# Decoder layer with contextual position attention: logits halved between transposes, distances on ScalarE, the window in the ring banks

## The reference, cut to what matters

```python
sim = einsum('bid,bjd->bij', q, k) * d ** -0.5
G = sigmoid(sim)
P = flip(cumsum(flip(G, -1), -1), -1)          # sum of the gates from here to the last key
P = minimum(P, 63)
E = einsum('bnc,ct->bnt', q, pos_emb)          # 64 table entries for each query
w = P - floor(P)
sim = sim + w * take(E, ceil(P)) + (1 - w) * take(E, floor(P))
out = einsum('bij,bjd->bid', softmax(sim), v)
```

## Time and profile before

| | us |
|---|---|
| median of 3 runs | 2650.29 (2649.49 to 2651.93) |
| profiled execution, its own time | 2652.94 |
| its span, first to last instruction | 2651.1 |
| mean granted TensorE clock | 0.985 |

### The profile page before, as it was taken

One profiled execution on the slowest core, in us unless ns is written; L12 is line 12 of the kernel. 1 busy time (PEld: TensorE's weight loads), 2 busy tenths in 40 slices (PEclk: granted clock), 3 DMA queues, 4 the chain that ended last, 5 costly groups with the idle time before them and its releaser, 6 DMA issues. The chain is left out here.

```text
span 2651.1 us, 64197 instructions
## 1 busy us (share of the span) xinstructions
PE 2472.1 (93%) x18687; PEld 1691.1 (64%) x18687; DVE 2006.4 (76%) x5179; ACT 1615.9 (61%) x3383; POOL 190.4 (7%) x289
## 2 busy tenths in 40 slices
PE   7999998999899989998999999999999988999997
PEld 5666665666566656666666566666666656777776
DVE  6888888888888888888888888888899960232322
ACT  4666666666666666666666666666666663444442
POOL 0000000000000000000000000000000000111111
PEclk9999999999999999999999999999999998999998
DMA  2010101010101010100101110101001002100100
GB/s 68 20 33 20 34 20 32 20 34 20 32 20 34 20 32 21 32 21 21 29 24 29 25 29 24 29 24 29 22 21 40 21 17 68 34 26 34 36 26 6
DMA packets 96567, 74.74 MB, mean 28 GB/s; under 512 B 24590, under 2 KB 92303, under 8 KB 96464
## 3 DMA queue, kind: packets, MB, share of 16 engines
q1 hardware_dynamic: 96464, 73.15, 10.1%
HBM read 14.26 MB, written 2.10 MB: 6 GB/s over the span
## 5 line engine op out<-in xcount | busy, mean ns | idle before, releaser
L748 DVE TENSOR_REDUCE mx<-Sc 128x1 f32<-128x1024 f32 x512 | 621.5, 1214 | 160.2 <-PE Sc L544 159.7
L552 PE MATMUL ring<-ident,probs 128*128 128x128 f32 x4096 | 620.9, 284 | 115.2 <-ACT attn L418 65.3
L409 ACT ACTIVATE probsT<-ring 128x512 f32<-128x512 f32 x1024 | 584.7, 596 | 132.1 <-PE ring L552 129.2
L552 PEld LDWEIGHTS ring<-ident,probs 128*128 128x128 f32 x4096 | 446.3, 145 | 258.3 <-ACT attn L418 127.0
L430 ACT ACTIVATE probs<-Sc,nbias 128x1024 f32<-128x1024 f32 x512 | 565.6, 1117 | 4.7 <-DVE nbias L765 4.7
L544 PE MATMUL Sc<-qk,q_now 64*128 64x512 f32 x2048 | 539.4, 637 | 22.4 <-issue 16.0
L566 PE MATMUL out<-probsT,V_now 128*64 128x128 f32 x8192 | 530.0, 277 | 0.0
L566 PEld LDWEIGHTS out<-probsT,V_now 128*64 128x64 f32 x8192 | 439.5, 137 | 76.3 <-ACT probsT L409 57.9
L712 DVE COPY_PREDICATED z<-mask,z 128x224 f32<-128x224 int16 (+5 forms) x768 | 389.7, 507 | 34.4
L418 ACT ACTIVATE attn<-ring,rsum 128x64 f32 (+1 forms) x256 | 80.3, 314 | 436.5 <-PE ring L575 420.7
L544 PEld LDWEIGHTS Sc<-qk,q_now 64*128 64x128 f32 x2048 | 173.6, 188 | 217.8 <-issue 217.8
(11 more groups left out here) (116 smaller groups left out, 2301.8 us busy)
## 6 DMA issues: line engine op xcount, KB each, us to landing
q_now<-qk SPq DMA_DIRECT2D x256, 64.0 KB, 2.0
xv<-xT SPq DMA_DIRECT2D x113, 128.0 KB, 2.2
q_far<-qk SPq DMA_DIRECT2D x128, 64.0 KB, 1.9
V_now<-V SPq DMA_DIRECT2D x16, 512.0 KB, 3.2
at<-attn SPq DMA_DIRECT2D x16, 512.0 KB, 3.2
probs<-in_x_dram SPq DMA_DIRECT2D x4, 512.0 KB, 5.3
wqk<-in_L_attn_Wq_dram SPq DMA_DIRECT2D x32, 64.0 KB, 2.1
xin<-in_x_dram SPq DMA_DIRECT2D x16, 128.0 KB, 2.8
```

What stands on the lines that cost most here:

```text
L409: nc.scalar.activation(probsT[:, u, 4 * s:4 * s + 4, :], ring[k % 2][:, :].rearrange("p (t q) -> p t q", q=P), ACT.Copy).then_inc(slot_out, 1)
L552: last = nc.tensor.transpose(ring[k % 2][:, j * P:(j + 1) * P], probs[:, u, (4 * s + j) * P:(4 * s + j + 1) * P], ident[:, :])
L748: nc.vector.tensor_reduce(mx[:, u, half:half + 1], Sc[:, half * HALF:(half + 1) * HALF], AX.X, ALU.max).then_inc(dve_unit, 1)
```

## The change

1. **TensorE's order.** In each half of the body: half of the unit's logits, two sets of transposes (they need only the first half of the previous unit's exponentials), the other half of the logits, the turn, two more sets (`early_half`, `turn_and_late_half`).
2. **Banks.** `near` is gone. The window's two matmuls write the two ring banks, in front of unit 1's first logits, and wait until both are empty; the transposes behind them wait until ScalarE has read both. The turn gets a bank of its own (`turns`, with semaphores `turned` and `scaled`), so a body has 10 ring slots instead of 12.
3. **The window's operands.** Query tile 0 stays on array rows 64 to 127, tile 1 moves to rows 0 to 63, against a copy of the window's keys and table (`k_near`, loaded once a head, in its second body). `q_far` is two loads of 128 columns instead of one of 256.
4. **The distances.** ScalarE computes 1 + tanh (`steps`), after VectorE's scan the rounded position (`positions`) and the int16 distance (`distances`), three 128x352 operations. VectorE loses the rounding, the two floor scans, the distance and the clamp, and one of two last shifts; it gains one int16 mask (`even`). The fraction is taken from the even position.
5. **The table.** ScalarE writes it into `near_table_in`; GpSimd copies that to `z` (128x352), once the correction of the pair before is made (`start_table`).
6. **VectorE's order.** The shifts 6 to 2 now stand together ahead of unit 1's maxima instead of between them. At a head, SyncE issues `q_far` ahead of `V_now` instead of behind it.

```diff
-        near = pb("near", [P, BANK])
-        ring = [pb(f"ring{i}", [P, BANK]) for i in range(2)]
+        rings = pb("rings", [P, 2, BANK])
+        ring = [rings[:, i, :] for i in range(2)]
         out = pb("out", [P, BANK])
+        turns = pb("turns", [P, BANK])
...
-        near_win = near[:, 0:2 * (W + T)].rearrange("p (i w) -> p i w", w=W + T)[:, :, 0:W]
-        near_E = near[:, 0:2 * (W + T)].rearrange("p (i w) -> p i w", w=W + T)[:, :, W:W + T]
+        near_win = rings[:, :, 0:W]
+        near_E = rings[:, :, W:W + T]
...
-                sp.dma_start(q_far[C:P, :], queries(h, odd, t)).then_inc(far_in, 16)
+                for i in range(2):
+                    rows = slice(0, C) if i else slice(C, P)
+                    sp.dma_start(q_far[rows, :], queries(h, odd, t, i)).then_inc(far_in, 16)
+
+            def load_near(h):
+
+                sp.dma_start(k_near[:, h % 2, 0:W], qk[C:P, h % 2, 1, HALF - W:HALF]).then_inc(k_near_in, 16)
...
+            def start_table(c):
+
+                pool.wait_ge(near_out, c * 2 + 2)
+                if not (isinstance(c, int) and c == 0):
+                    wait_apart(pool, corr_done, c, waited)
+                nc.gpsimd.tensor_copy(z[:, 0, :, :], near_table_in[:, :, :]).then_inc(z_in, 1)
...
-            def near_table(c):
-                nc.scalar.activation(z[:, 0, :, W - T:W], near_E, ACT.Copy).then_inc(near_out, 1)
+                                     near_win, ACT.Tanh, scale=-0.5).then_inc(near_out, 1)
+
+            def steps(c):
+
+                act.wait_ge(near_out, c * 2 + 1)
+                nc.scalar.activation(passed[:, :, :], tanh[:, :, :], ACT.Identity,
+                                     bias=bias_one[:, :]).then_inc(step_in, 1)
+
+            def positions(c):
+
+                act.wait_ge(scanned, c * SC + SC)
+                nc.scalar.activation(rnd[:, :, :], behind[:, :, :], ACT.Identity, scale=TO_STEPS,
+                                     bias=bias_rnd[:, :]).then_inc(rounded, 1)
+
+            def distances(c):
+
+                act.wait_ge(rounded, c + 1)
+                nc.scalar.activation(dist[:, :, :], rnd[:, :, :], ACT.Identity, scale=2.0,
+                                     bias=bias_dist[:, :]).then_inc(dist_in, 1)
+
+            def near_table(c, first=False):
+                if not first:
+                    wait_apart(act, z_in, c, waited)
+                nc.scalar.activation(near_table_in[:, :, W - T:W], near_E, ACT.Copy).then_inc(near_out, 1)
...
-                at = Slots(first, proj)
+                at = Slots(proj)
+                if near:
+                    positions(g + 1)
                 if not first:
 
                     empty_halves(g - 1, 0)
-                    scale(g - 1, 0, base, at.turn0)
+                if near:
+                    distances(g + 1)
+                if not first:
                     transposed(1, base, at.last)
-                if near:
-                    act.wait_ge(corr_done, g + 1)
-                    near_table(g + 1)
+                    scale(g - 1, 0)
                 exps(g, 0)
-                if not first:
-                    empty_halves(g - 1, 1)
                 if proj:
                     project(g + PAIRS, not odd, base, at.qk, alone=not val)
                 if val:
                     values(g, base, at.values)
                 if not first:
-                    scale(g - 1, 1, base, at.turn1)
+                    empty_halves(g - 1, 1)
+                if far:
+                    near_tanh(g + 2)
+                    near_table(g + 2)
+                    steps(g + 2)
                 transposed(0, base, at.now)
-                if far:
-                    act.wait_ge(scanned, g * SC + (SC + 2))
-                    near_tanh(g + 2)
+                if not first:
+                    scale(g - 1, 1)
                 exps(g, 1)
...
                 for i in range(2):
-                    last = nc.tensor.matmul(near[:, i * (W + T):(i + 1) * (W + T)], q_far[C:P, i * P:(i + 1) * P],
-                                            qk[C:P, par, 1, HALF - W:QK], start=True, stop=True)
+                    rows = slice(0, C) if i else slice(C, P)
+                    keys = k_near[:, par, :] if i else qk[C:P, par, 1, HALF - W:QK]
+                    last = nc.tensor.matmul(rings[:, i, 0:W + T], q_far[rows, :], keys,
+                                            start=True, stop=True)
...
-            def turn(g, u, base, k):
+            def turn(g, u, evicted=True):
 
                 pe.wait_ge(halves_out, g * 2 + u + 1)
-                pe.wait_ge(slot_out, base + k - 1)
-                nc.tensor.matmul(ring[k % 2][:, 0:C], halves[:, u, :], fold[:, :],
-                                 start=True, stop=True).then_inc(slot_full, 1)
-
-            def body(g, odd, par, late=False, first=False, proj=True, val=True, far=True, far_par=None):
+                if evicted:
+                    wait_apart(pe, scaled, g * 2 + u, waited)
+                nc.tensor.matmul(turns[:, 0:C], halves[:, u, :], fold[:, :],
+                                 start=True, stop=True).then_inc(turned, 1)
+
+            def early_half(u, base, slots):
+
+                for s in range(2):
+                    transposes(u, base, slots, s)
...
+            def turn_and_late_half(g, u, base, slots, turned_unit, first=False, evicted=True):
+
+                if not first:
+                    turn(g, turned_unit, evicted)
+                for s in range(2, 4):
+                    transposes(u, base, slots, s)
...
                 logits(par, 0, 0)
                 if not first:
+                    early_half(1, base, at.last)
                     wait_apart(pe, exp_done, g * 4, waited)
                 logits(par, 0, 1)
                 if not first:
-                    turn(g - 1, 0, base, at.turn0)
-                    for s in range(4):
-                        transposes(1, base, at.last, s)
+                    turn_and_late_half(g - 1, 1, base, at.last, 0, evicted=not second)
                     outputs(g - 1, 1, base, at.last, tiles=range(FIRST))
                 if proj:
                     weights_at = (g // PAIRS) * 64 + 128 if val else H * 64 - 16
...
+                if far:
+                    wait_apart(pe, slot_out, base + at.now[0], waited)
+                    window(g + 2, par if far_par is None else far_par)
                 wait_apart(pe, exp_done, g * 4 + 1, waited)
                 logits(par, 1, 0)
+                if far:
+                    wait_apart(pe, near_out, g * 2 + 6, waited)
+                early_half(0, base, at.now)
                 wait_apart(pe, exp_done, g * 4 + 2, waited)
                 logits(par, 1, 1)
-                if not first:
-                    turn(g - 1, 1, base, at.turn1)
-                for s in range(4):
-                    transposes(0, base, at.now, s)
-                if far:
-                    pe.wait_ge(near_out, g * 2 + 4)
-                    window(g + 2, par if far_par is None else far_par)
+                turn_and_late_half(g - 1, 0, base, at.now, 1, first)
                 outputs(g, 0, base, at.now, empty=not first)
...
-            def round_positions(c):
+            def saturation(c):
 
                 after_scan(c, "scan 1")
-                nc.vector.tensor_scalar(rnd[:, :, :], twoP[:, :, :], 2.0 * T - 3.0, RND2,
-                                        ALU.min, ALU.add).then_inc(scanned, 1)
-                nc.vector.tensor_tensor(satmin[:, :], satmin[:, :], twoP[:, :, 0], ALU.min)\
-                    .then_inc(ramped, 1)
-
-            def scan_floors(c):
-
-                after_scan(c, "round")
-                for i in range(2):
-                    nc.vector.tensor_tensor_scan(flo[:, i, ::-1], twos[:, :], rnd[:, i, ::-1], RND2 - 2.0,
-                                                 ALU.add, ALU.min).then_inc(shifted, 1)
-
-            def distances(c):
-
-                after(c, "floor 1")
-                nc.vector.tensor_tensor(dist[:, :, :], ramp[:, :, :], flo[:, :, :],
-                                        ALU.subtract).then_inc(shifted, 1)
+                nc.vector.scalar_tensor_tensor(satmin[:, :], behind[:, :, 0], -1.0, satmin[:, :],
+                                               ALU.mult, ALU.min).then_inc(ramped, 1)
...
-                after(c, "distances")
+                dve.wait_ge(dist_in, c + 1)
+                nc.vector.tensor_scalar(even[:, :, :], dist[:, :, :], (4 << BITS) - 4, 1,
+                                        ALU.bitwise_and, ALU.bitwise_or).then_inc(shifted, 1)
...
-            def clamp(c):
-
-                nc.vector.tensor_scalar(cut[:, :, :], twoP[:, :, :], 2.0 * T - 3.0, 1.0,
-                                        ALU.min, ALU.add).then_inc(shifted, 1)
-
-            def fractions(c):
-
-                nc.vector.scalar_tensor_tensor(frac[:, :, :], flo[:, :, :], RND2, cut[:, :, :],
```

(41 more changed lines are left out.)

192 lines of the change are left out of this document (109 added, 83 removed).

## The result

The changed kernel takes **2520.3 us**, median of 4 runs (2518.0 to 2523.4), beside 2649.9 us of the kernel before (2648.3 to 2651.9): a ratio of 0.951, 95% interval 0.950 to 0.953, 130 us less. 2506 was predicted, with 2462 to 2558 as the range.

A forecast was written before the change was run, and what follows sets the result against it. TensorE's own work and ring waits were taken as the bound; a body would fall by 1.2 us to 15.4. Gains of 133, 7 and 7 us less 2.5 make 144.5, a median of 2506 us, range 2462 to 2558.

The forecast's parts named there:

- The four waits: TensorE's waits for ring evictions in a body: all go with split logits and the turn's own bank, 1.5 us.
- the circle: Path from start to start through TensorE and ScalarE's evictions, scaling and exponentials: sets the new body at 15.4 us.
- The window in pairs: The window's two matmuls run on different row halves of TensorE's array: 0.5 us instead of 0.9.
- The switches of form: Changes of TensorE's array form, 12 a body instead of 9: 0.1 us each, 0.3 us added.
- The floor: TensorE's own work in a changed body: 15.0 us, the least a body can take.
- Rival 3: Faster handovers of exponentials and evictions let TensorE's 15.0 us decide: 51 us less, 2455 us; chance 0.12.
- the tie: Behind the window, tanh and table take 1.4 us, TensorE reaches the third transposes' set after 1.46: no cost.
- The sum: Gains of 133, 7 and 7 us by kind of body, less 2.5 in the opening: 144.5 us.
- Rival 5: VectorE sets the pace if gaps and waits sum to over 3.1 us: body 15.8, 2554 us; chance 0.05.
- Window in series: The window's two matmuls follow one another despite different rows: 48 us more, 2554 us; chance 0.08.
- Late queries: Loads of `q_now` land after 2.7 us instead of 2.0: 36 us more, 2542 us; chance 0.12.
- Rival 4: Slower than before: `q_now` landing at 4.0 us makes a body 17.0 us, the kernel 2700; chance 0.03.

The follow-up runs named there:

- e4: Kernel before, with VectorE's new chain and ScalarE's `positions` and `distances`, TensorE's order, ring and near bank old: 2648.0 us, ratio 1.000.
- e12: Changed kernel, logits whole, scalings ahead of evictions, second set of transposes carrying the wait for the scaling in place of its ring wait: 2602.4 us.
- e1: Changed kernel, but TensorE runs all of a unit's logits, the turn, then four sets of transposes in a row: 2546.1 us.
- e2: Changed kernel, but both of the window's multiplications read the same 64 rows, one behind the other: 2566.2 us.
- e11: Changed kernel, projections' evictions between the first unit's two exponentials, and the second unit's scaling behind the exponentials: 2451.9 us.
- e5: Changed kernel, logits whole, scalings ahead of evictions, a separate instruction making the second set of transposes wait for the scaling: 2635.6 us.
- e10: Changed kernel, VectorE's shift by one moved from behind the second unit's bias to behind the other shifts: 2526.3 us.
- e3: Changed kernel with VectorE's old distance chain and without ScalarE's three distance operations; TensorE and banks as changed: 2810.4 us.
- e6: Changed kernel with ScalarE's two scalings of a turned tile behind the exponentials: 2530.4 us.
- e8: Changed kernel with two more wide VectorE operations, results unused, behind the bias of the body's second unit: 2557.7 us.

## Why the prediction was right, and where it was off

**What bounds the kernel** held: TensorE's order and its waits on the ring. e4 takes VectorE out as a bound of the kernel before (ratio 1.000).

**The four waits** went, and the reason given was in part wrong. The prediction named both causes, half of the logits between the sets and the turn's own bank, and sized them as one, 1.5 us. The bank is the larger: 0.45 us a body, the split 0.31 (e12, e1, the change). Beyond those the removed waits bought nothing, because the circle took over.

**The window in pairs**, 0.4 us: 0.50 start to start as forecast, and 0.39 by e2, 0.33 on the way up.

**The switches of form**, 0.1 each: in the changed kernel logits to turn take 1.06 us (1010.72 to 1011.78) where the half takes 0.98 when logits follow, so 0.08. The rule of the Trainium skill (TensorEngine Tiling (Array Packing), Key Properties), a drain at each switch, is not borne out as a drain to the modelled end of the last matmul: that end is at 1011.85, and the turn starts before it.

**The floor**, 15.0 us, was put too high: e11 runs at 14.96 with a short wait still in it, and at 14.75 in two bodies. The changed kernel stays above both. Rival 3's 15.0 and 2455 us are near what e11 reaches, with two more edits.

**The circle**, 8.4 + 7.05, was stated as 15.4: it is 8.36 + 7.15, 15.52 over the long stretch. The terms as written add up to 15.44, so 0.04 of the 0.12 is rounding. The step that slipped is the tie, "1.4 us in all" against TensorE's 1.46: tanh starts 0.71 after the window, the table's eviction ends 0.63 later, as added; but the handover to the transposes, taken as 0.1, is 0.29 (1009.42 to 1009.71). The transposes are late by 0.17 for that, and 0.07 came back along the rest. The prediction's own sign of being wrong, transposes that wait for the table by more than 0.1, is met: in the bodies where the handover takes 0.14, they start 1.01 us behind the logits, and in the others 1.12, so at least 0.11 of it is a wait. The window's handover was taken as 0.1 and is 0.29 too (1007.79 to 1008.08); the first half shows nothing of it, since its other steps are shorter by as much. The 0.29 is the instruction that waits with the register operation behind it, as in e5.

**The sum.** 144.5 us were forecast between the two profiled executions and 129.6 gained. Of the 15 missing, 11 are the body's 1.09 in place of 1.2. 2 are the outer loop's turns and the early bodies: 30 us over 112 times 15.52, before 28 over 112 times 16.61. The 8 bodies without values gave 5 and not 7, the late ones 3 and not 7: in these VectorE sets the pace (e10), which the prediction had not looked for. Against that, the opening gained half a microsecond where a loss of 2.5 was forecast, and the rest of the program behind the stage gained 1.

**ScalarE** is busy for 12.06 us a body, 12.3 forecast. The three new operations take 0.59 to 0.61 us each where tanh on the same 352 elements takes 0.46; from start to start two of them take 0.48 and 0.50 (1000.53 to 1001.01, 1001.17 to 1001.67), where 0.36 had been taken. It cost nothing that the rows show: behind them ScalarE still waits 1.0 us for the third set of transposes (1003.77).

**VectorE** is where the reasoning was wrong and the number right by luck. It was put at 12 to 12.5 us a body and is at 13.25 (1.5 us fewer, not 2.5). The summed lengths of its operations do fall by 2.3 us (17.3 to 15.0), but they overlap less: the five shifts in a row take 2.99 us from start to start (1007.01 to 1010.00) for 2.51 of length. Rival 5 let it decide only if its gaps summed to over 3.1 us. Its busy time says nothing of how near it was: by its own circle it stood 0.12 us from setting the pace (15.40; e3, e6 and e8 give 17.56, 15.59 and 15.87 by it, measured 17.58, 15.60 and 15.86). Had the chain been left as it was, the outcome would have been the slower one, 2810, through a cause to which the rivals gave 0.05 and 2554 us.

**The rivals.** Window in series: not so, and priced right (48 us forecast, 46 in e2). Late queries: TensorE waited for `q_now` 7 times in the first 112 bodies, 7.0 us, the longest 2.0, where 36 were priced; in the stretch of 12 bodies never. Rival 4 did not come.

TensorE's waits from the start to 1810 us of the changed kernel:

```profile
PE rings L581 <- ACT V L412: 41.1, 112, 2.4
PE Sc L607 <- ACT probs L484: 23.9, 98, 0.6
PE Sc L607 <- issue: 16.4, 7, 3.5
PE Sc L607 <- DMA q_now<-qk: 7.0, 7, 2.0
```
